# Global attention of 16 heads: heads laid at 32 rows each, scores also computed key-major, exponentials written turned

## What is computed

```python
h = _layernorm(x, axis=-1) * (1 + ca) + sa
q = (h @ Wq.T + bq).reshape(b, s, HEADS, HEAD_DIM)
...
q = q * SCALE
scores = jnp.einsum('bqhd,bkhd->bhqk', q, k)
probs = jax.nn.softmax(scores, axis=-1)
out = jnp.einsum('bhqk,bkhd->bqhd', probs, v).reshape(b, s, d)
x = x + ga * (out @ Wo.T + bo)
h = _layernorm(x, axis=-1) * (1 + cb) + sb
```

## Time and profile before

| | us |
|---|---|
| median of 3 runs | 5793.53 (5793.14 to 5795.39) |
| the profiled execution | 5792.16 |
| its span in the profile | 5790.3 |
| phase A, first scores to its last write | 54.6 to 689.8 |
| mean TensorE clock granted over the span | 0.962 |

### The profile page before, as it was taken

How to read it: one execution, slowest core, us unless ns; L and a number is a source line. 1 busy time by engine, 2 the same in 40 slices (tenths; PEclk the granted TensorE clock), 3 DMA queues, 4 the chain that set the end, 5 groups by cost and what they waited for, 6 DMA issues and landing times. The chain is left out here.

```text
span 5790.3 us, 112187 instructions
## 1 busy us (share of the span) xinstructions
PE 5207.9 (90%) x34984; PEld 3808.2 (66%) x34984; DVE 4944.2 (85%) x8818; ACT 4116.4 (71%) x12293; POOL 3339.1 (58%) x2277
## 2 busy tenths in 40 slices
PE   7999899999999999999999999999999996667666
PEld 6999766776676766767767666677676774333333
DVE  4666689999999999999999999999999994787877
ACT  3555478888788788788888887878878785544543
POOL 1222266666666666676666766766667662443444
PEclk9999899999999999999999999999999997788887
DMA  1000000000000000000000000000000000000000
GB/s 21 4 4 3 24 1 1 0 0 10 11 0 0 0 13 8 0 0 6 14 1 0 0 6 15 0 0 0 10 5 0 0 0 5 1 3 3 2 3 4
DMA packets 35422, 25.54 MB, mean 4 GB/s; under 512 B 11315, under 2 KB 29302, under 8 KB 35190
## 3 DMA queue, kind: packets, MB, share of 16 engines
q1 hardware_dynamic: 26302, 22.22, 1.3%
q10 hardware_dynamic: 8888, 0.45, 0.1%
HBM read 20.57 MB, written 2.10 MB: 4 GB/s over the span
## 5 line engine op out<-in xcount | busy, mean ns | idle before, releaser
L1145 POOL TENSOR_TENSOR b_w<-b_w,b_vt 128x512 f32<-128x512 f32 x768 | 980.0, 1276 | 1276.8 <-DVE b_vt L1054 646.6
L1149 POOL TENSOR_TENSOR b_rn<-b_ssm,all_neg_half 128x16 f32<-128x16 f32 x384 | 1126.9, 2935 | 32.0
L971 ACT ACTIVATE b_PT<-ps 128x512 f32<-128x512 f32 x768 | 461.0, 600 | 434.4 <-PE ps L826 433.7
L1080 DVE TENSOR_REDUCE b_nm<-ps 128x4 f32<-128x640 f32 x768 | 631.0, 822 | 95.1 <-PE ps L806 85.2
L953 ACT ACTIVATE b_Pr<-ps,b_nm 128x128 f32<-128x128 f32 x1536 | 564.0, 367 | 179.0 <-DVE b_nm L1080 176.6
L874 PE MATMUL ps<-b_Whi,b_xlo 128*128 128x512 f32 x1152 | 584.7, 508 | 40.9 <-DVE b_vt L1054 27.9
L955 ACT ACTIVATE b_Pr<-ps,b_nm 128x160 f32<-128x160 f32 x1536 | 610.0, 397 | 0.0
L1052 DVE TENSOR_TENSOR b_w<-ps,until_b_rotab 128x512 f32<-128x512 f32 x768 | 529.4, 689 | 25.0 <-ACT b_sq L986 7.5
L986 ACT ACTIVATE b_sq<-ps 128x512 f32<-128x512 f32 x768 | 467.1, 608 | 82.3 <-PE ps L876 81.9
L1054 DVE TENSOR_TENSOR b_vt<-ps,until_b_rotab 128x512 f32<-128x512 f32 x768 | 523.2, 681 | 0.0
L1056 DVE TENSOR_REDUCE b_ss<-b_sq 128x8 f32<-128x512 f32 x768 | 519.7, 677 | 0.0
(11 more groups left out here) (256 smaller groups left out, 13996.5 us busy)
## 6 DMA issues: line engine op xcount, KB each, us to landing
b_Wraw<-in_L_ffn_Wqkv SPq DMA_DIRECT2D x36, 256.0 KB, 2.8
b_Wo<-in_L_ffn_Wo SPq DMA_DIRECT2D x6, 512.0 KB, 4.0
a_xtok<-in_L_attn_hidden_states SPq DMA_DIRECT2D x16, 128.0 KB, 2.1
out<-c_xout SPq DMA_DIRECT2D x16, 128.0 KB, 1.8
b_W<-in_L_ffn_W SPq DMA_DIRECT2D x6, 341.0 KB, 2.9
setup_wmod<-in_L_wmod SPq DMA_DIRECT2D x2, 384.0 KB
b_W<-in_L_ffn_W SPq DMA_DIRECT2D x6, 128.0 KB
setup_rot<-in_rot SPq DMA_DIRECT2D x1, 256.0 KB
```

What stands on the lines that cost most here:

```text
L1080: nc.vector.tensor_reduce(s.nm[:, 2 * p:2 * p + 2], ps[:, S_BANK[0]:S_BANK[1] + 1, 0:TT * KEYS].rearrange("p j (t k) -> p j t k", t=TT), A ...
L1145: nc.gpsimd.tensor_tensor(rows, rows, s.vt[:, i % 4], ALU.add).then_inc(s.pool_add, 1)
L1149: nc.gpsimd.tensor_tensor(s.rn[:, j], s.ssm[:, j], g.neg_half[:, 0:HB], ALU.pow).then_inc(s.pool_r, 1)
```

## The change

A head gets 32 rows of its own: `wq4` and `wk4` are the weights spread so that a projection of 128 output rows yields four heads (a quad), each with one spare row and its eight rows of q or k. The spare row of k is 1 (from the bias tile `bqk4`), that of q is first 0. A step now has four places `at`, one for a quad.

- For each quad the scores are computed twice. Query-major, two heads at a time (`scores`), each matmul over its 32 rows: DVE takes one maximum over two banks, 128 by 1024 elements, into `nmz`, which is zero elsewhere. PE turns `nmz` and DVE adds it to `q4`, which puts the negated maximum into the spare row. Key-major, all four heads into four banks: these scores have the maximum already taken off, and ACT writes their exponentials (four of 128x512, without a bias or a sum) to `PT`, which is the layout that the product with V needs.
- V is laid out at 32 columns a head with a column of ones, so that the product (PE, 32 output rows a head, four heads in one bank) also yields the sums. ACT copies it, PE turns it, DVE divides.
- Gone are `qm` and its multiplications on POOL, the four transposes of a head, the copies of the turned probabilities, the reads of the accumulator, and `head_rows`.
- The q and k projections are now eight matmuls of 256 columns for a sequence (two before), and DVE instead of ACT writes them. `layernorm_apply_c` runs on ACT with a shift that POOL computes, one step earlier than before for the first layer norm. ACT instead of DVE writes V, `g.x2T` and `s.x2tok`; the residual and the second layer norm of a sequence are one step later.
- Setup loads `bqk4` with eight transfers from ACT's queue instead of the three of `bqk` and `head_rows`, and these wait for four memsets on POOL instead of one. Phase A begins with memsets of `nmz` and `V` on DVE.
- Two banks, `A_BANK` and `B_BANK`, are shared by all small jobs. The loop runs ten steps.

The diff, cut to its core (16 heads of 8 features, `HROWS` is 32):

```diff
-        small += [(g.bqk[:, 0:1], flat(d["L0_attn_bq"])), (g.bqk[:, 1:2], flat(d["L0_attn_bk"])), (g.head_rows[:], d["head_rows"])]
+        for at, name in enumerate(("L0_attn_bq", "L0_attn_bk")):
+            for j in range(4):
+                small.append((g.bqk4[32 * j + 1:32 * j + 1 + D0, at], d[name].rearrange("(i r) -> r i", i=4)[D0 * j:D0 * (j + 1)]))
...
-            nc.gpsimd.memset(g.lparam[:], 0.0).then_inc(s.consts, 1)
+            nc.gpsimd.memset(g.lparam[:], 0.0)
+            nc.gpsimd.memset(g.bqk4[:], 0.0)
+            nc.gpsimd.memset(g.wq4[:], 0.0)
+            nc.gpsimd.memset(g.wk4[:], 0.0).then_inc(s.consts, 1)
...
+class LayerNormC(LayerNorm):
...
+def layernorm_stats_c(nc, dve, ln, src, n):
...
+    nc.vector.tensor_tensor(ln.var[:], ln.mv[:, :, 1], ln.var[:], ALU.add)
+    nc.vector.tensor_scalar_mul(ln.negm[:], ln.mv[:, :, 0], -1.0).then_inc(ln.var_ready, 1)
+
+
+def layernorm_pool_c(nc, pool, ln, g, n):
+    pool.wait_ge(ln.var_ready, n + 1)
+    nc.gpsimd.tensor_tensor(ln.rstd[:], ln.var[:], g.neg_half[:, 0:TT], ALU.pow).then_inc(ln.rstd_ready, 1)
+    pool.wait_ge(ln.rstd_ready, 2 * n + 1)
+    nc.gpsimd.tensor_tensor(ln.shift[:], ln.negm[:], ln.rstd[:], ALU.mult).then_inc(ln.rstd_ready, 1)
+
+
+def layernorm_apply_c(nc, act, ln, src, n):
+
+    act.wait_ge(ln.rstd_ready, 2 * n + 2)
+    for tt in range(TT):
+        last = nc.scalar.activation(ln.xn[:, tt], src[:, tt], ACT.Identity, bias=ln.shift[:, tt:tt + 1], scale=ln.rstd[:, tt:tt + 1])
+    last.then_inc(ln.normed, 1)
...
+        s.q4 = s.sb("q4", [P, 2, QUADS, NT]); s.k4 = s.sb("k4", [P, 2, QUADS, NT])
+        s.V = s.sb("V", [P, 2, TT, H0, HROWS])
+        s.nmz = s.sb("nmz", [P, 2, TT, GROUP, HROWS])
+        s.PT = s.sb("PT", [P, GROUP, TT, NT]); s.OT = s.sb("OT", [P, NT])
...
+        S_BANK, ST_BANK, A_BANK, B_BANK = (0, 1), (2, 3, 4, 5), 6, 7
...
+        def quad(step, at, lag):
+
+            if at >= lag:
+                return (step.n, at - lag, step.odd) if step.heads else (None, None, None)
+            return (step.n - 1, at - lag + QUADS, 1 - step.odd) if step.tail else (None, None, None)
...
+            nc.vector.memset(s.nmz[:], 0.0)
+            nc.vector.memset(s.V[:], 0.0).then_inc(s.prepared, 1)
+            dve.wait_ge(s.prepared, 1)
+            nc.vector.memset(s.V[:, :, :, :, D0:D0 + 1], 1.0).then_inc(s.prepared, 1)
...
+                def maxima(at, pair):
+                    dve.wait_ge(s.s_done, 2 * (QUADS * n + at) + pair + 1)
+                    nc.vector.tensor_reduce(s.nmz[:, at % 2, :, 2 * pair:2 * pair + 2, 0].rearrange("p t j -> p j t"),
+                                            ps[:, S_BANK[0]:S_BANK[1] + 1].rearrange("p j (t k) -> p j t k", t=TT),
+                                            AX.X, ALU.max, negate=True).then_inc(s.max_done, 1)
...
+                    if step.last and at == 0:
+                        dve.wait_ge(s.proj_full, u + 1)
+                        dve.wait_ge(s.md_last_ready, u + 1)
+                        nc.vector.tensor_scalar(s.tmp[:], ps[:, A_BANK, 0:NT], g.bo[:], s.md_out[:], ALU.add, ALU.mult).then_inc(s.tmp_ready, 1)
+                    if step.early and at == 3:
+                        dve.wait_ge(s.x_in[step.odd], 16 * known(e >> 1) + 16)
+                        layernorm_stats_c(nc, dve, s.l1, s.xtok[:, step.odd], e)
...
+                        maxima(at, 0)
+                    item, i, parity = quad(step, at, 1)
+                    if item is not None:
+                        dve.wait_ge(s.nm_full, QUADS * item + i + 1)
+                        nc.vector.tensor_tensor(s.q4[:, parity, i], ps[:, A_BANK, 0:NT], s.q4[:, parity, i], ALU.add).then_inc(s.nm_ready, 1)
+                    if step.last and at == 0:
+                        dve.wait_ge(s.tmp_ready, u + 1)
+                        nc.vector.tensor_tensor(s.x2s[:], s.tmp[:], g.x2T[:, bass.ds(u_at, NT)], ALU.add).then_inc(s.x2s_ready, 1)
+                    if step.heads:
+                        maxima(at, 1)
+                    item, i, parity = quad(step, at, 2)
+                    if item is not None:
+                        dve.wait_ge(s.o_full, QUADS * item + i + 1)
+                        both = ps[:, A_BANK, 0:NT].rearrange("p (t g r) -> p t g r", t=TT, g=GROUP)
+                        nc.vector.reciprocal(s.rinv[:], both[:, :, :, D0]).then_inc(s.recip, 1)
+                        dve.wait_ge(s.recip, QUADS * item + i + 1)
+                        nc.vector.tensor_tensor(s.o[:, parity, :, GROUP * i:GROUP * (i + 1)], both[:, :, :, 0:D0],
+                                                s.rinv[:].rearrange("p t (g o) -> p t g o", o=1).broadcast_to((P, TT, GROUP, D0)), ALU.mult).then_inc(s.o_ready, 1)
+                    if step.front:
+                        dve.wait_ge(s.qk_full, QUADS * f + at + 1)
+                        nc.vector.tensor_scalar(s.q4[:, pf, at], ps[:, B_BANK, 0:NT], float(D0) ** -0.5, g.bqk4[:, 0, at:at + 1], ALU.mult, ALU.add)
+                        nc.vector.tensor_scalar(s.k4[:, pf, at], ps[:, B_BANK, NT:2 * NT], g.bqk4[:, 1, at:at + 1], None, ALU.add).then_inc(s.qk_ready, 1)
+                    if step.last and at == 1:
+                        dve.wait_ge(s.x2tok_ready, u + 1)
+                        layernorm_stats_c(nc, dve, s.l2, s.x2tok, u)
...
-                        for tt in range(TT):
-                            last = nc.scalar.activation(s.Pr[:, h % 4, tt], ps[:, S_BANK[h % 2], tt * NT:(tt + 1) * NT], ACT.Exp,
-                                                        bias=s.nm[:, h, tt:tt + 1], accum_out=s.ssum[:, step.odd, h, tt:tt + 1])
...
+                for at in range(QUADS):
+                    if step.last and at == 2:
+                        layernorm_apply_c(nc, act, s.l2, s.x2tok, u)
+                    if step.early and at == 3:
+                        layernorm_apply_c(nc, act, s.l1, s.xtok[:, step.odd], e)
+                    item, i, parity = quad(step, at, 2)
+                    if item is not None:
+                        act.wait_ge(s.pv_done, QUADS * item + i + 1)
+                        nc.scalar.activation(s.OT[:], ps[:, B_BANK, 0:NT], ACT.Copy).then_inc(s.ot_ready, 1)
+                    if step.front and at == 0:
+                        act.wait_ge(s.md_front_ready, f + 1)
+                        act.wait_ge(s.hx_full, f + 1)
+                        nc.scalar.activation(s.hT[:], ps[:, B_BANK, 0:NT], ACT.Identity, bias=s.md_front[:, 0:1], scale=s.md_front[:, 1:2])
+                        nc.scalar.activation(g.x2T[:, bass.ds(f_start, NT)], ps[:, B_BANK, NT:2 * NT], ACT.Copy).then_inc(s.hT_ready, 1)
...
+                    item, i, parity = quad(step, at, 1)
+                    if item is not None:
+                        act.wait_ge(s.st_done, QUADS * item + i + 1)
+                        for j in range(GROUP):
+                            last = nc.scalar.activation(s.PT[:, j], ps[:, ST_BANK[j]].rearrange("p (k t) -> p k t", k=TT), ACT.Exp)
+                        last.then_inc(s.exp_done, 1)
+                    if step.last and at == 0:
+                        act.wait_ge(s.x2_full, u + 1)
+                        nc.scalar.activation(s.x2tok[:], ps[:, A_BANK, 0:NT].rearrange("p (t e) -> p t e", t=TT), ACT.Copy).then_inc(s.x2tok_ready, 1)
+                    if step.front and at == 1:
+                        act.wait_ge(s.v_full, f + 1)
+                        nc.scalar.activation(s.V[:, pf, :, :, 0:D0], ps[:, A_BANK, 0:NT].rearrange("p (t h e) -> p t h e", t=TT, e=D0), ACT.Copy).then_inc(s.v_ready, 1)
...
+                def scores(i, pair):
+
+                    pe.wait_ge(s.qk_ready, QUADS * n + i + 1)
+                    wait(pe, s.max_done, 2 * (QUADS * n + i) + pair)
+                    for tt in range(TT):
+                        for j in range(2):
+                            r = rows_of(2 * pair + j)
+                            last = nc.tensor.matmul(ps[:, S_BANK[j], tt * NT:(tt + 1) * NT], s.q4[r, pa, i, tt * P:(tt + 1) * P], s.k4[r, pa, i],
+                                                    start=True, stop=True, skip_group_check=True)
+                    last.then_inc(s.s_done, 1)
...
+                def wait_a(at):
+
+                    older, k, _ = quad(step, at, 3)
+                    if older is not None:
+                        pe.wait_ge(s.o_ready, QUADS * older + k + 1)
+                    if step.last and at == 0:
+                        pe.wait_ge(s.tmp_ready, u + 1)
+                    if step.last and at == 1:
+                        pe.wait_ge(s.x2tok_ready, u + 1)
+                    if step.front and at == 2:
+                        pe.wait_ge(s.v_ready, f + 1)
+                    if step.tail and at == 3:
+                        pe.wait_ge(s.oT_ready, t + 1)
...
+                for at in range(QUADS):
                     if step.heads:
-                        h = slot
-                        if h == 0:
```

(43 more changed lines are left out.)

308 lines of the change are left out of this document (118 added, 190 removed).

## The result

Measured beside each other, the changed kernel takes 5648.5 us (median of 4 runs, 5646.0 to 5668.6) and the kernel before 5794.1: a ratio of 0.9746, 95% interval 0.971 to 0.9782. The forecast was 5613.5, with 5565 to 5709 as its range. So the sign and the main size are right, and 35 us of the 180 that I expected are missing.

What follows compares the result with a forecast made beforehand. PE's gapless stream bounds phase A; afterwards PE, DVE and ACT form one chain. Edges of 125 us plus 14 steps of 27.5 end phase A at 510, 180 us earlier: 5613.5 us, range 5565 to 5709.

Steps and rivals of the forecast that it cites:

- Four tiles at once, 0.85 a group: Phase A, PE: four 32-row or 32-column tiles run at once, so key-major scores or values take 0.85 us a group.
- rival 1: Phase A: only two tiles run at once, or waits were missed; step 34.3 us, kernel 5709 us; chance 0.16.
- rival 3: Phase A: tiles of 32 do not overlap at all; step 54.8 us, kernel 5996 us; chance 0.03.
- Step 27.5: Phase A: one step takes 27.5 us, from 26.0 walked plus 1.5 for dearer changes of form.
- the walk's places: Phase A: the four places of a step, walked through PE, DVE and ACT, take 7.1, 6.5, 5.9 and 6.5 us.
- Place 1: Second place of a step: 6.5 us, with the turned maximum waiting for `x2tok` and V's projection adding 0.9.
- Place 0: First place of a step: 7.1 us, with DVE's modulation and `tmp` ahead of the maximum, which ends at 3.07.
- The first step: Phase A's first step: 23.5 us without tail, plus 3 for the slow clock of the first place.
- The end: End of phase A: 20.5 us for the last step without front, then 18 to drain.
- Rival 2, the clock: Phase A: PE's clock falls; slower kernel, 5869 us if throughout; chance 0.03 slower, 0.02 no change; partly slow shares 0.05.
- the x of the forecast: Share of phase A's steps at 1.2 GHz; a step takes 27.5 + 17.5x us, no gain at x = 0.73.
- "Phases B and C as long as before": Phases B and C: untouched, so predicted to stay at 4167.5 and 932.6 us.

Runs made afterwards that it cites:

- the last reordering: Changed kernel with V's one-row matmuls first, fill matmuls, and place 0's L429 behind the first maximum, turned maxima behind the second scores: 5617.5 us, 0.9694.
- The fill matmuls: Changed kernel plus extra matmuls whose results nobody reads, in the first front and the first two places of the first heads: 5638.8 us, 0.9728.
- the fastest kernel: Changed kernel with V's one-row matmuls first, fill matmuls and place 0 reordered: 5617.5 us, 0.9694; shifted by 31 small matmuls and a transpose: 5625.5 us.
- The second profile: Another profiled execution of the changed kernel without any edit, span 5648.1 us; that run measured 5649.9 us, 0.9753.

## Why the prediction was right, and where it was off

- **Four tiles at once, 0.85 a group** (from pairs in phase B): right. 1.00 to 1.07 with the change of form, and the runs with two and with one row group price the alternatives: rival 1 would have cost 0.68 a group by the step (I said 0.85), rival 3 2.8 a group at full clock (I said 2.6) and the clock on top, which I had not coupled to it. Both runs price the key-major scores alone; for the product with V, whose tiles lie side by side in columns, four at once is shown by its 1.00 us.
- **Step 27.5**: 27.32 to 27.56, but partly by luck, since errors cancel. With 0.17 for each change of form the walk's places are 7.5, 6.9, 6.3 and 6.9; measured 7.1 to 7.25, 7.3, 6.4 and 6.5. Place 1 is longer for V's projection, mis-sized at 0.9 for 1.66: I counted records and left out the changes between one-row and full matmuls. Reordering them gave 0.4 back. Place 0 is not bound by DVE's L429, as the last reordering shows; what holds it is open.
- **Edges**: first scores at 61.6, 60 forecast. **The first step failed**: 35.7, where the sum had 26.5 (23.5, and 3 for the slow clock). I took it that PE comes to full clock as soon as it is busy, as it did before. It stayed at half for 26 us. The fill matmuls took 10 us off this step and show the cause; which property of these small matmuls and transposes leaves the clock low is not shown.
- **The end**: from the last step's start to the barrier 45.0, forecast 38.5. The drain is a chain of single operations, each of which waits for the one before on another engine, and its last 14 us are at half clock; I had priced it at full. The clock explains the lesser part: a pair of transposes takes 0.69 there where it took 0.41, and by such rows I estimate under 2 of the 6.5 us. No run splits the rest further.
- **DVE and ACT**: maximum 1.22 (1.22 forecast), exponential 0.60 (0.60), layer-norm tile on ACT 0.49. DVE 70% busy, as forecast.
- **Rival 2, the clock**: in full steps there was no stretch at half clock in one profile and five in the other, 3.1 us each, 16 in all. There the x of the forecast is about 0.06.
- **"Phases B and C as long as before" failed**, by 19 and 4 us, the largest single term. The step was "B and C are not touched and begin behind a barrier, so what phase A gives, the program gives". B's code was the same, its place in PE's instruction stream wasn't. Shifting the kernel before alone gives 17 of the 19 in its profile, some 12 by the medians; shifting the changed one back takes 14 off. The 5 that remain, and why place 169 is worse than 41, 88, 105 or 218, are open. In the changed kernel and all that are built on it a second instruction queue carries 261 or 262 packets (114 before, 115 before shifted), and their phase B is never under 4172.6; no run separates its cost. Of C's 4 us, the changed kernel shifted back shows 0.3 (932.9) and the fastest kernel shifted 4.0 (936.6). Over all these kernels C took 931.6 to 938.4: open too.

The second profile in a sum, against the forecast: first scores +1.6, first step +9.2, fourteen steps -2.5, last step and drain +6.5: 524.7 for 510. With +19.4 and +3.9 that is 38 over the forecast's span of 5610.1.

## What to carry to other kernels

A change of code moves everything behind it in each engine's instruction stream. Where a long loop turns back, compare the idle time and the clock at its back edge between two profiles before explaining a difference in untouched code; here it was worth 0.3%, and it hid in the gain of two other experiments. And price a group of small matmuls by form: alternating one-row and full ones cost as much as the products themselves, while four 32-row tiles side by side are nearly four times as fast.

## What the hardware showed beyond what I expected

- **Tiles overtake each other.** All of L541 stands before L621 in the program, yet L621 began at 308.04 while the second pair of L541 went on to 308.50, in other rows of the array. That the order of the tiles in pairs changed nothing fits this.
- **A busy PE can be granted half the clock.** 6.80 of 6.80 us busy at 0.50, and with one row group 51.20 of 51.20 at 0.67, while the same products on four row groups ran at 1.00 with 3.4% of idle time.
- **The turn of a long loop can bring the clock down.** At place 169 a stretch at half clock, mostly of 6.8 us, stood at 27 of the 28 turns of those profiles; elsewhere 5 of 28 had one, of 3.4 us. The idle time right at the turn does not decide it alone: it was 1.53 to 3.29 us at place 169 and 1.39 to 1.96 elsewhere. But at place 169 a second idle time followed some 3 us later at 21 of the turns, elsewhere at none, and the two together are 2.25 to 4.74 us there. What the waits cost and what the clock costs can be told apart. First a turn of the kernel with V's one-row matmuls first, then one of the kernel with one row group, the only turn at place 169 without a stretch (PE's timeline, then windows):

```profile
2749.05 0.44 PE L901 MATMUL ps<-until_b_mask_bf,until_b_ident_bf 128*128 128x320 bf16 x2 [1.81 <-issue]
...
2752.45 0.79 PE L976 MATMUL ps<-b_Whi,b_xlo 128*128 128x512 f32 x1 [0.65 <-issue]
...
2749.50:2756.20 6.70, 6.05 (x28) 4.21 (x29) 4.41 (x8) 2.65 (x10) 0.00 (x0) 0.50 0.02 7
```

```profile
2447.22 0.44 PE L900 MATMUL ps<-until_b_mask_bf,until_b_ident_bf 128*128 128x320 bf16 x2 [1.55 <-issue]
...
2450.36 0.49 PE L975 MATMUL ps<-b_Whi,b_xlo 128*128 128x512 f32 x1 [1.41 <-issue]
...
2446.00:2456.00 10.00, 7.37 (x58) 5.43 (x58) 6.64 (x12) 5.54 (x17) 1.76 (x2) 1.00 0.03 7
```

The layer of the first, with 2.46 us idle and the stretch, took 689.6 us; that of the second, with 2.96 idle and full clock, 687.6. Without a stretch the turns elsewhere have layers of 686.5 in the mean. So the longer waits alone cost about 1.1 us and the stretch the larger part, some 2 to 3.
